# The columns of a widened source tile padded from 490 to 512, so that a matmul of the layers fills a whole PSUM bank

## The chip, the cores and the metric

The kernel runs on one core of one Trainium2 chip. The metric is the device time of one execution in microseconds; lower is better. The kernel before takes 4031.41 us (median of 3 runs, 4030.12 to 4032.72).

## What is computed

Two graph networks with a residual and a layer norm behind each. The change sits in the first, three graph convolutions on 6250 nodes and 200000 edges that are sorted by destination:

```python
def _graph_conv(x, W, b, src, dst, norm_src, norm_dst, n_nodes, act):
    h = x @ W
    m = h[src] * norm_src[:, None]
    agg = jax.ops.segment_sum(m, dst, num_segments=n_nodes)
    out = agg * norm_dst[:, None] + b
    return jax.nn.relu(out) if act else out
...
h = _graph_conv(feats, W1, b1, src, dst, norm_src, norm_dst, n, act=True)
h = _graph_conv(h, W2, b2, src, dst, norm_src, norm_dst, n, act=True)
h = _graph_conv(h, W3, b3, src, dst, norm_src, norm_dst, n, act=False)
...
x = _layernorm(x + _L0_gnn_ref(...), axis=-1)
```

The second network works per edge (two dense layers on a basis of the edge's weight, then a running product over the edges of a node) and comes behind the layers; the change does not touch it.

## The kernel before

The program has stages with a barrier between them: a stage that counts, a stage with the three layers, a stage on the edges, and a short end.

**What the layers work on.** The counting stage leaves a table of step counts in memory: for each of 49 source tiles of 128 nodes and each of 7840 steps (a step gathers up to 128 edges of one destination), how often each source node occurs in that step. Its entries are small whole numbers in bf16. One layer sums, for every step, the scaled node rows by these counts: a matrix product of `hp` (the node rows, 128 nodes x 128 features per source tile, as weights) with the counts (128 nodes x steps, moving). The steps are cut into `BLOCKS` = 16 blocks of `SB` = 490, the source tiles into `NG7` = 7 groups of 7. The counts of one block and one group, 7 tiles of 490 columns, are a **granule**; a layer has 112 of them, three layers 336.

**How a granule goes through.** SyncE loads it as bf16 into `gran`, a ring of 7 (`load_granule`, L738). Two engines widen it to 4 bytes (fp32r) into `wide`, a ring of `WIDE` = 2: VectorE its first `NEAR` = 4 tiles in one instruction (`widen`, L990), ScalarE the other 3 (`widen`, L823). TensorE then runs 14 matmuls (`granule`, L900): for each of the 7 tiles one for each of `PARTS` = 2 parts of `hp` (a rounded part and the rest that rounding leaves, so that the product keeps its precision). All 98 matmuls of a block add into one PSUM bank, `ybanks[n.parity()]`, of which 490 of the 512 columns are used. `s_un` says that the near tiles are used, `s_gran` that the granule is; on these VectorE and ScalarE wait before they write the slot again. `s_wn` and `s_wf` say that a slot is widened; on these TensorE waits.

**Behind a block.** VectorE scans the 490 sums into segment sums (L960), scales them (L964) and adds the bias (L969); TensorE multiplies by the layer's weights (`times_w`, L911, four fp32 matmuls of 128 columns, issued behind the first granule of the next block); ScalarE copies and stores the rows (L806, L813). GpSimd gathers each node's last row for the next layer (L796), VectorE scales it (L982), and ScalarE and VectorE split it into the two parts of `hp` (L829, L994). The opening of a layer runs granules of two blocks in an order of its own (`LEAD`), so that TensorE has work while the last node rows come in.

A row of `wide` for one tile is 490 x 4 = 1960 bytes long before and the next begins right behind it; tile 0 of slot 0 begins where the ring begins, which is the same place before and after.

Of the kernel before, what the change touches and what calls it, by code (L numbers as in the profile page):

```python
# [7 lines left out]
F32 = mybir.dt.float32  # L8
BF16 = mybir.dt.bfloat16
F32R = mybir.dt.float32r  # L10
# [4 lines left out]
P = 128  # L15
# [14 lines left out]
SB = 490  # L30
# [8 lines left out]
WIDE = 2  # L39
# [26 lines left out]
def gnn(nc, x, src, dst, edge_attr, edge_weight, w1, b1, w2, b2, w3, b3, v1, c1, v2, c2, v3, c3, out):  # L66
# [14 lines left out]
    with outer:  # L81
# [35 lines left out]
        with ExitStack() as ph:  # L117
            sbt = sb_in(ph)
# [104 lines left out]
            with nc.Block() as block:  # L223
# [263 lines left out]
                def _(act):  # L487
                    done = [0]

                    def tables(j):  # L490

                        n = RB[j + 1] - RB[j]
                        act.wait_ge(s_lo, j + 1)
                        if j:
                            act.wait_ge(s_tf, fills_to[j - 1])
                        nc.scalar.copy(lo_b[:, 0:n, :], lo_i[:, 0:n, :]).then_inc(s_lob, 1)
                        while done[0] < fills_to[j]:
                            f = done[0]
                            _, tab, a, b = fills[f]
                            act.wait_ge(s_tf, f + 1)  # L500
                            turned, n = banks[4 + f % TBANKS][:, 0:(b - a) * P], (b - a) * P
                            if tab == 0:
                                nc.scalar.copy(lo_t[:, a * P:b * P], turned).then_inc(s_te, 1)
                            else:
                                nc.scalar.copy(hi_t[:, a * P:b * P, :], turned.unsqueeze(2).to_broadcast([P, n, 2])  # L505
                                               ).then_inc(s_te, 1)
                            done[0] += 1
# [28 lines left out]
                def _(pe):  # L536
# [32 lines left out]
                    def turn_tables(j):  # L569

                        pe.wait_ge(s_lob, j + 1)
                        pe.wait_ge(s_hib, j + 1)
                        while done[0] < fills_to[j]:
                            f = done[0]
                            _, tab, a, b = fills[f]
                            if f >= TBANKS:
                                pe.wait_ge(s_te, f - TBANKS + 1)
                            for t in range(a, b):
                                last = nc.tensor.matmul(banks[4 + f % TBANKS][:, (t - a) * P:(t - a + 1) * P],
                                                        (lo_b, hi_b)[tab][:, t - RB[j], :], ident_b[:],  # L580
                                                        start=True, stop=True)
                            last.then_inc(s_tf, 1)
                            done[0] += 1
# [49 lines left out]
        with ExitStack() as ph:  # L633
            sbt = sb_in(ph)
            hps = sbt("hp", [P, NT, PARTS, D], F32R)
            hps_f = hps[:].bitcast(F32)
            gran = sbt("gran", [P, RING, 7, SB], BF16)
            wide = sbt("wide", [P, WIDE, 7, SB], F32R)
            by_tile = lambda ring, i, a, b: ring[:, i % RING, :, a * IS:b * IS].rearrange("p i (t s) -> p t i s", s=IS)
            in_runs = lambda i, a, b: wide[:, i % WIDE, a:b, 0:SB].rearrange("p t (i s) -> p t i s", s=IS)  # L640
            x_again = sbt("x_again", [P, 2, 7, D])
# [12 lines left out]
            ybanks, rbanks = banks[0:2], banks[2:4]  # L654
# [66 lines left out]
            def gathered(engine, q, k, last_too):  # L721
                early = 7 if q < 6 else LATE - 42
                engine.wait_ge(s_xg[q], 16 * early * k)
                if q == 6 and last_too:
                    engine.wait_ge(s_xl, 16 * (NT - LATE) * k)

            with nc.Block() as block:
# [159 lines left out]
                @block.tensor  # L887
                def _(pe):
                    def granule(k, n, g, i=None):
                        if g == 0:  # L890
                            pe.wait_ge(s_scan, n.value(1, 1))
                        y, r = ybanks[n.parity()][:, 0:SB], (n.parity() + g) % WIDE if i is None else i % WIDE
                        nth = n.value(7, g + 1) if i is None else i + 1
                        pe.wait_ge(s_wn, nth)
                        for t in range(7):
                            if t == NEAR:
                                pe.wait_ge(s_wf, nth)
                            for part in range(PARTS):
                                first, last_ = (g, t, part) == (0, 0, 0), (g, t, part) == (6, 6, PARTS - 1)
                                last = nc.tensor.matmul(y, hps[:, 7 * g + t, part, :], wide[:, r, t, :],  # L900
                                                        start=first, stop=last_)
                            if t == NEAR - 1:
                                last.then_inc(s_un, 1)
                        last.then_inc(s_gran, 1)

                    def times_w(k, m):
                        pe.wait_ge(s_scaled, m.value(1, 1))
                        pe.wait_ge(s_ho, m.value(1, 1))
                        rows = rbanks[m.parity()]
                        for t, a in enumerate((0, P, 2 * P, SB - P)):  # L910
                            last = nc.tensor.matmul(rows[:, t * D:(t + 1) * D], scaled[:, a:a + P], ws[k][:],  # L911
                                                    start=True, stop=True)
                        last.then_inc(s_z, 1)

                    pe.sem_inc(s_z, 1)

                    def one_block(k, n):
                        for g in range(NG7):
                            granule(k, n, g)
                            if g == 0:  # L920
                                times_w(k, n.plus(-1))

                    def opening(k):
                        for i, (b, g) in enumerate(LEAD):
                            if b == 0:
                                pe.wait_ge(s_hp, NG7 * k + g + 1)
                            granule(k, At(BLOCKS * k + b), g, NG7 * BLOCKS * k + i)
                            if i == 0:
                                times_w(k - 1, At(BLOCKS * k - 1))
                            if i == FIRST_DONE:  # L930
                                times_w(k, At(BLOCKS * k))

                    for k in range(3):
                        if k == 0:
                            for g in range(NG7):
                                pe.wait_ge(s_hp, g + 1)
                                granule(0, At(0), g)
                            pe.wait_ge(s_w, 16 * 6)
                            one_block(0, At(1))
                        else:  # L940
                            opening(k)
                        with pe.Fori(0, (BLOCKS - 2) // 2) as it:
                            for h in range(2):
                                one_block(k, At(BLOCKS * k + 2 + h, it, 2))
                    times_w(2, At(BLOCKS * 3 - 1))

                @block.vector
                def _(dve):
                    links = [0]

                    def link(ins):
                        links[0] += 1
                        ins.then_inc(s_link3, 1)
                        dve.wait_ge(s_link3, links[0])
# [23 lines left out]
                    def scale_h(k, q):  # L978
                        part = x_sb[:, 7 * q:7 * q + 7, :]
                        if k:  # L980
                            gathered(dve, q, k, True)
                        nc.vector.tensor_tensor(part, part, norm_src[:, 7 * q:7 * q + 7].unsqueeze(2).to_broadcast([P, 7, D]),  # L982
                                                ALU.mult).then_inc(s_hm, 1)
# [53 lines left out]
                    def normalise(i):  # L1037
# [4 lines left out]
                                                           ALU.subtract, ALU.mult)  # L1042
                        last.then_inc(s_x1, 1)

                    scale_h(0, 0)
                    scale_h(0, 1)
                    rest_h(0, 0)
# [62 lines left out]
        with ExitStack() as ph:  # L1110
            sbt = sb_in(ph)
# [310 lines left out]
        with ExitStack() as ph:  # L1422
            sbt = sb_in(ph)
# [168 lines left out]
```

## Time and profile before

| | |
|---|---|
| median of 3 runs | 4031.41 us (4030.12 to 4032.72) |
| the profiled execution: its own time | 4028.69 us |
| its span | 4026.8 us |
| mean granted TensorE clock over the span | 0.879 |
| TensorE busy | 3234.2 us, 80% of the span |
| matmuls of L900 | 4704 |
| time from the first to the last of them | 850.7 to 1945.0 us of the span |

The page gives busy time by engine, then 40 equal slices of the span (some 100.7 us each) with the busy tenths of each engine and the granted clock. The layers lie in slices 9 to 19. A busy TensorE is not a TensorE at its peak: matmuls are pipelined, a record lasts longer than the distance to the next one, and what a matmul costs is read from where one begins to where the next begins. A weight load (PEld) is recorded as beginning together with the matmul that runs beside it; its records are shorter than a matmul's turn in the layers, so the timeline can show them one by one, and the distance between two weight loads is read as the distance between two matmuls.

### The profile page before, as it was taken

The page shows a single profiled execution, that of the slowest core. Times are in us where ns is not written, and L with a number is a line of the kernel's source. Part 1 is how long each engine was busy: PE and PEld are TensorE (multiplying, and loading weights), DVE is VectorE, ACT ScalarE, POOL GpSimd, SP SyncE. Part 2 cuts the span into 40 slices and gives each one's busy share as a digit, 9 for nine tenths or more (in the row PEclk, how much of TensorE's full clock was granted, in tenths as well). Part 3 has the DMA queues.
Part 4 walks back from the last instruction along what each step waited for, and adds up shares of the span by engine and source line. Part 5 has one row for each costly group of instructions (what it writes and reads, how often), then busy time and mean ns, then how long its engine had stood idle before and what let it go on. Part 6 is the DMA issues. An engine that isn't in the chain of part 4 may idle for free. (4 is left out here: it accounts for less than half of the span.)

```text
span 4026.8 us, 61194 instructions
## 1 busy us (share of the span) xinstructions
PE 3234.2 (80%) x21477; PEld 2643.9 (66%) x21477; DVE 3228.0 (80%) x5075; ACT 2856.6 (71%) x3090; POOL 1934.6 (48%) x1883
## 2 busy tenths in 40 slices
PE   4898888879999999999677777777777777777763
PEld 3777777768888888888456555555555555555542
DVE  9999999964555545555599989898889889898896
ACT  3666666654445445444599999999999999999973
POOL 6122200042210121021477777777777777777774
PEclk7888888899999999999888888888888888888885
DMA  4444333379999999999587877777777777777762
GB/s 136 135 134 132 129 124 130 131 259 317 321 307 318 311 314 318 303 340 321 171 221 217 221 209 209 209 212 207 210 211 212 209 216 207 211 209 210 209 170 77
DMA packets 363341, 876.56 MB, mean 218 GB/s; under 512 B 54730, under 2 KB 213695, under 8 KB 363175
## 3 DMA queue, kind: packets, MB, share of 16 engines
q1 hardware_dynamic: 272471, 739.80, 57.5%
q0 software_dynamic: 59936, 119.71, 13.0%
q10 hardware_dynamic: 30768, 15.26, 1.3%
q8 instruction: 54, 0.88, 0.1%
q14 instruction: 112, 0.92, 0.1%
HBM read 653.46 MB, written 221.09 MB: 217 GB/s over the span
## 5 line engine op out<-in xcount | busy, mean ns | idle before, releaser
L1199 POOL DMA_INDIRECT hgat<-x_rows,edge_src x1564 | 1476.0, 944 | 485.5 <-issue 484.9
L900 PE MATMUL psum<-wide,hp 128*128 128x490 f32 x4704 | 1060.6, 386 | 15.5 <-DVE wide L990 14.2
L900 PEld LDWEIGHTS psum<-wide,hp 128*128 128x128 f32 x4704 | 884.5, 189 | 173.6 <-issue 15.1
L823 ACT CAST wide<-gran 128x1470 fp32r<-128x1470 bf16 x336 | 479.4, 1427 | 547.2 <-PE psum L900 538.7
L990 DVE CAST wide<-gran 128x1960 fp32r<-128x1960 bf16 x336 | 397.6, 1184 | 439.3 <-PE psum L900 431.8
L609 PEld LDWEIGHTS psum<-hi_hot,lo_hot 128*128 128x128 bf16 x7840 | 544.5, 155 | 216.4 <-issue 66.7
L1380 DVE TENSOR_SCALAR psum<-rows_e,edge_same,edge_first 128x128 f32<-128x128 f32 x1564 | 644.2, 412 | 42.4
L525 ACT CAST stage<-psum 128x490 bf16<-128x490 f32 x784 | 451.1, 575 | 306.3 <-PE psum L609 297.8
L609 PE MATMUL psum<-hi_hot,lo_hot 128*128 128x49 bf16 x7840 | 572.8, 219 | 93.4 <-DVE hi_hot L401 91.8
L1304 PE MATMUL psum<-c_b,one_b 96*128 96x512 bf16 x391 | 186.4, 477 | 507.1 <-DVE prod_e L1362 503.4
L796 POOL DMA_INDIRECT x_sb<-h_rows,last_i x147 | 179.7, 1223 | 856.3 <-DMA h_rows<-h_out 822.5
L1308 PEld LDWEIGHTS psum<-v_sb,excess 128*128 128x128 f32 x3128 | 543.9, 245 | 28.1
L398 DVE TENSOR_TENSOR lo_hot<-lo_t,rep_lo 128x8960 bf16<-128x8960 bf16 x112 | 539.4, 4816 | 5.0 <-ACT hi_t L505 4.5
L1308 PE MATMUL psum<-v_sb,excess 128*128 128x128 f32 x3128 | 537.0, 328 | 0.0
L1308 PE MATMUL psum<-v_sb,a 128*128 128x128 f32 x3128 | 513.8, 319 | 0.0
L1383 DVE TENSOR_TENSOR rows_e<-psum,prod_e 128x128 f32<-128x128 f32 x1564 | 455.1, 291 | 53.4
L1308 PEld LDWEIGHTS psum<-v_sb,a 128*128 128x128 f32 x3128 | 483.6, 235 | 0.0
L1304 PEld LDWEIGHTS psum<-c_b,one_b 96*128 96x128 bf16 x391 | 44.2, 113 | 666.0 <-DVE prod_e L1362 319.5
L1293 PE MATMUL psum<-dist,v_sb 128*128 128x512 f32 x782 | 374.4, 601 | 47.3 <-ACT dist L1225 25.5
L560 PE MATMUL psum<-stage,ident_b 128*128 128x490 bf16 x791 | 343.0, 435 | 0.2 <-ACT stage L525 0.2
L1256 ACT ACTIVATE a<-psum,soft_max 128x1024 f32<-128x1024 f32 x196 | 217.6, 1110 | 141.4 <-PE psum L1308 140.9
L1362 DVE TENSOR_TENSOR prod_e<-hgat,psum 128x1024 f32<-128x1024 f32 x196 | 238.8, 1218 | 87.4 <-issue 73.1
(218 smaller groups left out, 3667.7 us busy)
## 6 DMA issues: line engine op xcount, KB each, us to landing
gran<-step_counts SPq DMA_DIRECT2D x336, 857.5 KB, 6.6
dist<-weight_by_step SPq DMA_DIRECT2D x195, 512.0 KB, 6.7
running_products<-rows_e SPq DMA_DIRECT2D x195, 512.0 KB, 3.2
step_counts<-stage SPq DMA_DIRECT2D x112, 857.5 KB, 5.1
ef<-in_edge_attr SPq DMA_DIRECT2D x195, 448.0 KB
hgat<-x_rows,edge_src POOLq DMA_INDIRECT x1564
kn<-keep_and_norm_of_steps SPq DMA_DIRECT2D x48, 490.0 KB, 8.0
ef<-in_edge_attr SPq DMA_DIRECT2D x171, 64.0 KB
```

Of the source, the lines that this page charges most:

```text
L398: nc.vector.tensor_tensor(lo_hot[:, r], lo_of.unsqueeze(2).to_broadcast([P, 7, P, GS]), rep_lo[:].unsqueeze(1).to_broadcast([P, 7, P, GS]) ...
L525: nc.scalar.copy(stage[:, u % 2, :, g * GS:(g + 1) * GS], banks[f % 4][:, 0:GS * NT].rearrange("p (s h) -> p h s", h=NT)).then_inc(s_ev, 1)
L560: return nc.tensor.matmul(counts, ident_b[:], stage[:, r, :, g * GS:(g + 1) * GS], start=False, stop=False)
L609: last = nc.tensor.matmul(banks[f % 4][:, s * NT:(s + 1) * NT], lo_hot[:, u % 2, g, :, s], hi_hot[:, u % 2, g * GS + s, 0:NT], start=True, ...
L823: nc.scalar.copy(in_runs(i, NEAR, 7), by_tile(gran, i, NEAR, 7)).then_inc(s_wf, 1)
L900: last = nc.tensor.matmul(y, hps[:, 7 * g + t, part, :], wide[:, r, t, :], start=first, stop=last_)
L990: nc.vector.tensor_copy(in_runs(i, 0, NEAR), by_tile(gran, i, 0, NEAR)).then_inc(s_wn, 1)
L1199: pool.indirect_dma_start(out=hgat[:, f % U, c, :], out_offset=None, in_=x1_d, in_offset=bass.IndirectOffsetOnAxis(ap=edge_src[:, 2 * f + ...
L1293: last = nc.tensor.matmul(ps1[:, a:a + BLK], v1_sb[:], dist[:, f.ring(Q), a:a + BLK], start=True, stop=True)
L1308: last = nc.tensor.matmul(z[:, at:at + D], part[:, f.parity(), at:at + P], v2_sb[:], start=False, stop=part is a1 and c == C4 - 1)
L1380: nc.vector.tensor_scalar(factors[:, c], before, edge_same[:, b, c:c + 1], edge_first[:, b, c:c + 1], ALU.mult, ALU.add).then_inc(s_fac, 1)
L1383: nc.vector.tensor_tensor(rows_e[:, r, e, :], factors[:, c], prod_e[:, f % R, e, :], ALU.mult).then_inc(s_row if c < C4 - 1 else s_run, 1)
```

## The change

The rows of `wide` get 512 columns in place of 490. The last 22 of each of the 14 rows are set to zero once, by one VectorE instruction at the start of the layers; the widening goes on writing columns 0 to 489 only. `y` becomes the whole bank, and since the matmul takes `wide[:, r, t, :]`, it takes 512 columns in and writes 512. What reads the bank (L960) still reads 490 columns.

```diff
@@ -635,7 +635,7 @@
             gran = sbt("gran", [P, RING, 7, SB], BF16)
-            wide = sbt("wide", [P, WIDE, 7, SB], F32R)
+            wide = sbt("wide", [P, WIDE, 7, 512], F32R)
             by_tile = lambda ring, i, a, b: ring[:, i % RING, :, a * IS:b * IS].rearrange("p i (t s) -> p t i s", s=IS)
             in_runs = lambda i, a, b: wide[:, i % WIDE, a:b, 0:SB].rearrange("p t (i s) -> p t i s", s=IS)
@@ -889,7 +889,7 @@
                         if g == 0:
                             pe.wait_ge(s_scan, n.value(1, 1))
-                        y, r = ybanks[n.parity()][:, 0:SB], (n.parity() + g) % WIDE if i is None else i % WIDE
+                        y, r = ybanks[n.parity()], (n.parity() + g) % WIDE if i is None else i % WIDE
                         nth = n.value(7, g + 1) if i is None else i + 1
@@ -1042,6 +1042,7 @@
+                    link(nc.vector.memset(wide[:, :, :, SB:512].bitcast(F32), 0.0))
                     scale_h(0, 0)
                     scale_h(0, 1)
                     rest_h(0, 0)
```

No instruction changes its place. On VectorE, at the start of the layers, one instruction is added ahead of the first scaling of the node rows (L982), and the widening writes four runs of 490 where it wrote one of 1960:

```order
 L1005 MEMSET soft_max 128x1
 L1006 TENSOR_SCALAR center<-pcol 128x1
+L1045 MEMSET wide 128x14x22
 L982 TENSOR_TENSOR x_sb<-x_sb,norm_src 128x896 x2
 L994 TENSOR_TENSOR hp<-x_sb,hp 128x7x128
-L990 CAST wide<-gran 128x1960 x2
+L990 CAST wide<-gran 128x4x490 x2
```

The widening by ScalarE (L823) changes in the same way, from one run of 1470 to three of 490. On TensorE, at the start of the first layer, the count of the matmuls stays and their width changes:

```order
 L887 UNCONDITIONAL_BRANCH
-L900 MATMUL psum<-wide,hp 128x490 x112
+L900 MATMUL psum<-wide,hp 128x512 x112
 L911 MATMUL psum<-w,scaled 128x128 x4
-L900 MATMUL psum<-wide,hp 128x490 x84
+L900 MATMUL psum<-wide,hp 128x512 x84
```

So it goes on through all three layers.

## Rows read from the trace of the kernel before

**Rows 1.** The page: busy time of TensorE, and its 40 slices.
```profile
PE 3234.2 (80%) x21477; PEld 2643.9 (66%) x21477; DVE 3228.0 (80%) x5075; ACT 2856.6 (71%) x3090; POOL 1934.6 (48%) x1883
...
PE   4898888879999999999677777777777777777763
...
PEclk7888888899999999999888888888888888888885
```

**Rows 2.** Windows, the layers behind their first eight granules: busy time by engine, clock.
```profile
core 0: us, PE busy (x) PEld busy (x) DVE busy (x) ACT busy (x) POOL busy (x), PEclk, DMA share, GB/s
883.00:1945.00 1062.00, 1062.00 (x4959) 906.93 (x4958) 558.70 (x627) 506.60 (x389) 208.31 (x169) 1.00 0.93 315
```

**Rows 3.** Groups of instructions, 1000 to 1800 us, shapes apart.
```profile
line engine op names shapes xcount | busy us, mean ns | idle before us <-releasers
L900 PE MATMUL psum<-wide,hp 128*128 128x490 f32 x3457 | 777.9, 386 | 0.0
...
L823 ACT CAST wide<-gran 128x1470 fp32r<-128x1470 bf16 x247 | 352.4, 1427 | 398.1 <-PE psum L900 398.1
L990 DVE CAST wide<-gran 128x1960 fp32r<-128x1960 bf16 x247 | 292.2, 1184 | 330.2 <-PE psum L900 329.9
...
L994 DVE TENSOR_TENSOR hp<-x_sb,hp 128x896 fp32r<-128x896 f32 x14 | 15.3, 1091 | 13.7 <-ACT hp L829 13.7
...
L829 ACT CAST hp<-x_sb 128x896 fp32r<-128x896 f32 x14 | 13.2, 943 | 12.6 <-PE psum L900 10.9 <-DVE x_sb L982 1.8
```

**Rows 4.** Waits, 880 to 1945 us: who waited for whom, total, times, longest.
```profile
ACT wide L823 <- PE psum L900: 532.4, 315, 1.9
DVE wide L990 <- PE psum L900: 431.8, 252, 2.3
```

**Rows 5.** Timeline of weight loads: tile 0, then tile 1 of a slot-0 granule; next two granules.
```profile
1206.67 0.19 PEld L900 LDWEIGHTS psum<-wide,hp 128*128 128x128 f32 x1
1207.11 0.19 PEld L900 LDWEIGHTS psum<-wide,hp 128*128 128x128 f32 x1
1209.80 0.19 PEld L900 LDWEIGHTS psum<-wide,hp 128*128 128x128 f32 x1
1212.90 0.19 PEld L900 LDWEIGHTS psum<-wide,hp 128*128 128x128 f32 x1
```

**Rows 6.** Timeline of weight loads: second and sixth matmul of the layers, clock 0.50.
```profile
851.25 0.33 PEld L900 LDWEIGHTS psum<-wide,hp 128*128 128x128 f32 x1
852.88 0.33 PEld L900 LDWEIGHTS psum<-wide,hp 128*128 128x128 f32 x1
```

**Rows 7.** Windows of L900 alone, around those of group 6 (its columns: PE, PEld, PEclk).
```profile
851.20:853.30 2.10, 2.10 (x7) 1.66 (x6) 0.50 1.03 422
```

**Rows 8.** Timeline of weight loads, edge stage: two matmuls with 512 columns.
```profile
2989.37 0.19 PEld L1293 LDWEIGHTS psum<-dist,v_sb 128*128 128x128 f32 x1 [0.24 <-issue]
2989.80 0.19 PEld L1293 LDWEIGHTS psum<-dist,v_sb 128*128 128x128 f32 x1 [0.24 <-issue]
```

**Rows 9.** Windows, all engines, around those of group 8: the clock.
```profile
2988.00:2990.90 2.90, 2.82 (x14) 1.51 (x13) 2.73 (x7) 2.90 (x4) 1.99 (x4) 1.00 0.92 219
```

**Rows 10.** Timeline of VectorE at the start of the layers.
```profile
845.08 2.09 DVE L982 TENSOR_TENSOR x_sb<-x_sb,norm_src 128x896 f32<-128x896 f32 x2
847.32 1.10 DVE L994 TENSOR_TENSOR hp<-x_sb,hp 128x896 fp32r<-128x896 f32 x1
849.38 1.18 DVE L990 CAST wide<-gran 128x1960 fp32r<-128x1960 bf16 x1 [0.96 <-DMA gran<-step_counts]
```

**Rows 11.** Groups of VectorE's memsets: the two nearest in size.
```profile
L389 DVE MEMSET stage<- 128x1715 uint32 x1 | 1.5, 1488 | 0.3 <-issue 0.3
L1387 DVE MEMSET c_b<- 96x256 uint32 x1 | 0.3, 272 | 0.0
```

**Rows 12.** Timeline of TensorE: the first eight granules of the layers.
```profile
850.70 7.79 PE L900 MATMUL psum<-wide,hp 128*128 128x490 f32 x28 [12.80 <-DVE wide L990]
858.91 6.49 PE L900 MATMUL psum<-wide,hp 128*128 128x490 f32 x28 [0.43 <-DVE hp L994]
865.84 6.50 PE L900 MATMUL psum<-wide,hp 128*128 128x490 f32 x28 [0.44 <-DVE hp L994]
872.77 3.39 PE L900 MATMUL psum<-wide,hp 128*128 128x490 f32 x14 [0.42 <-DVE hp L994]
877.53 3.35 PE L900 MATMUL psum<-wide,hp 128*128 128x490 f32 x14 [1.37 <-DVE wide L990]
```

## The prediction, made before the changed kernel ran

> **What bounds the kernel now.** I began with the page [rows 1]. The change touches the layers alone; in its slices 10 to 19 TensorE is busy for nine tenths or more and its clock is granted in full. Next came the windows of that stage [rows 2]: from 883 to 1945 us TensorE is busy for 1062.00 of 1062.00 us, at clock 1.00 (2.4 GHz), while VectorE has 558.70 and ScalarE 506.60 us of work. Third the groups and waits [rows 3, 4]: the matmuls of L900 have no idle time before them, and both widening engines wait for these matmuls, 431.8 us in VectorE's case and 532.4 us in ScalarE's. So the stage lasts as long as its matmuls, and each nanosecond on one of the 4704 is a nanosecond on the end: behind the stage is a barrier, and nothing of the edge stage can start earlier.
>
> **What one matmul costs now.** A matmul's record (386 ns) is longer than its turn, so I read starts. In [rows 5] a granule of slot 0 begins at 1206.67 us, the next (slot 1) at 1209.80 and the third at 1212.90. That is 6.23 us for 28 matmuls, or **222.5 ns** each. Its columns alone are 490 / 2.4 GHz = 204.2 ns. So each matmul has some **18.3 ns** that no column explains. At the start of the stage the clock is 0.50 (1.2 GHz) [rows 7], and there four matmuls take 852.88 - 851.25 = 1.63 us [rows 6], 407.5 ns each. The columns alone are 490 / 1.2 GHz = 408.3 ns there, so at half clock the surplus is gone. Two things follow: columns are paid one by one (490 are not rounded up to 512, which would be 427 ns), and the surplus belongs to something that only shows at full clock. What that is no row tells, and the forecast turns on what it does at 512 columns.
>
> **The change part by part.**
>
> *Twenty-two columns more in each of 4704 matmuls.* If the surplus stays as it is, a matmul costs 22 / 2.4 GHz = 9.17 ns more, 231.7 ns, and all of them 4704 x 9.17 = **43.1 us**. If it grows with the columns (a stream that comes in at a slower rate than one column per cycle), a matmul costs 222.5 x 512 / 490 = 232.5 ns, 10.0 ns more: 47.0 us. If it is gone at 512, the nearest row with that width sets the end: L1293 at full clock moves 512 columns of fp32, two cycles for each, from 2989.37 to 2989.80 us [rows 8, 9], 0.43 us, where 1024 cycles are 0.427 us; 3 ns of surplus. By that a matmul of L900 would cost 213.3 + 3 = 216 ns, 6.5 ns less than now: 4704 x 6.5 = 30.6 us off. I take 43.1 us: the row at half clock is of the same instruction and shows columns paid one by one, while L1293 reads its columns at half the speed, so the surplus of L900 need not show there in any case.
>
> The Trainium skill's page "TensorE: Matmul & The Clock Gate", section "Back-to-back issue gap", speaks against that choice: it gives N / 2.4 + 2.5 ns for one matmul behind another, and 215.7 ns as measured at 512 columns. For 490 columns that rule makes 206.7 ns, which [rows 5] does not bear out (222.5); for 512 it makes 215.8 ns and so 4704 x 6.7 = 31.5 us off, were the padded rows to run by it.
>
> *The first eight granules.* These are 112 of the 4704 matmuls, and TensorE waits between them for node rows and for loaded granules [rows 12]. What they lengthen (112 x 9.17 = 1.0 us) can partly go into those waits: between 0 and 1.0 us of the 43.1. I leave it in.
>
> *One memset of 14 x 22 = 308 columns, and a wait for it.* [Rows 11] give 272 ns for 256 columns and 1488 ns for 1715, so some 0.85 ns a column: about 0.32 us, at most twice that for short runs and the wait. It delays L982 and L994 behind it, but L990 then waits 0.96 us for the first granule's load [rows 10], and the first matmul needs L990. Cost 0; if the load came earlier, at most 0.6 us.
>
> *Widening into runs of 490.* L990 takes 1184 ns and L823 1427 ns [rows 3], of a granule's 3.1 us. Writing with gaps is seen on L829, 943 ns for 896 elements, 1.05 ns each against L823's 0.97: at that rate L823 takes 1.55 us. For VectorE the bad end is the pace of L994 (1091 / 896 = 1.22 ns): L990 would take 2.39 us, 1.2 us more. VectorE waits 431.8 / 336 = 1.29 us a granule for TensorE [rows 4], so even that is covered on average, and 336 x 1.2 = 403 us on its 558.70 leaves it at 962 of 1062 us. Cost 0; the bad end is priced below. The granules' loads change by nothing: TensorE takes them 4% more slowly.
>
> Sum: +43.1 us on the profiled execution's 4028.69 us is 4071.8 us. The median of the runs lies 2.7 us above that execution, so for the median I say 4031.41 + 43.1 = **4074.5 us**, 1.07% slower.
>
> **The rivals.**
>
> *A, the forecast: columns are paid.* 43.1 us, with bounds 34 (alignment gives back 2 ns of 9) and 47: 4065 to 4079 us.
>
> *B, the surplus comes from rows that begin anywhere, and goes.* Tiles are 1960 bytes apart now, so of the 14 rows of the ring most begin off any larger boundary; padded to 2048 bytes all begin alike. If the read of a row that begins badly costs the 18.3 ns, the change ends at 216 ns a matmul: 4031.41 - 30.6 = 4000.8 us. It turns to a gain once more than 9.2 of the 18.3 ns go. For it: the surplus is real, shows only at full clock, where columns are read fastest, and the two slots differ (3.13 and 3.10 us, [rows 5]), as they also do in where their rows begin. Against it: tile 0 of slot 0 already begins where it begins after the change, and its two matmuls take 1207.11 - 1206.67 = 0.44 us, 220 ns each; a well-placed start saves some 2 ns, not 18. The loads can follow that pace too: DMA's share of 0.93 would be 0.96 [rows 2]. The Trainium skill's page "SBUF — State Buffer", section "Specifications (TRN2)", has a rule for this rival: memory is read in lines of 16 bytes and each step to a new line costs something. Half of the rows begin inside such a line now, none afterwards; [rows 5] shows no such step at tile 0.
>
> *C, the 512 columns are there already.* If whatever feeds the array works in pieces of 64 or 128 columns, 490 cost it as much as 512 at full clock, and the surplus is the rest of the last piece: 222.5 ns stay, 4031.4 us. For it: 512 / 2.4 = 213.3 ns plus a few for the start comes near 222.5, and at half clock the array, not the feed, would be the limit, as [rows 6] has it. Against it: no row shows steps by pieces.
>
> *D, VectorE loses its pace* in L990 and is late behind each block, where L960, L964 and L969 also stand: 48 blocks with up to 1 us each on top of A, up to 4122 us. For it: the output is no longer one run. Against it: the 1.29 us of waiting per granule.
>
> That the change does not do what it says I set aside: the matmuls have 512 columns in all three layers.
>
> **How the numbers follow.** A 0.74, B 0.12, C 0.11, D 0.03. The predicted time is A's. A's own range is 4065 to 4079 us; with up to 5 us for casts that are now and then late, 4084. A alone is less than 8 in 10, so the range goes down to take in C with its scatter, 4028 us; B and D are left out. A change below 0.2% (8 us) cannot be told from none here: faster is B, 0.12; same is C, 0.11; slower A and D, 0.77.
>
> **What would show it.** Right: the distance of matmuls of L900 near 231.7 ns (3.24 us a granule) at clock 1.00, the span from first to last grown by 43 us, TensorE without gaps, the waits of VectorE and ScalarE for L900 longer by some 40 us each, L990 and L823 as long as before, and stages before and behind unchanged. Wrong: a distance near 216 ns (B) or 222.5 ns (C), or idle time before L900 put down to L990 (D).

## The result

| | median, us | ratio to before, 95% interval |
|---|---|---|
| before | 4031.55 (4030.12 to 4032.72, 4 runs) | |
| the change | 4084.76 (4084.43 to 4086.60, 4 runs) | 1.0132 [1.0120, 1.0144] |

The change costs 53.2 us. Forecast were 43.1 us, and a range that ended at 4084.0 us. The sign and the mechanism were right, a term of some 10 us was missing, and the time lies 0.8 us above the end of the range.

### The profile page after: what moved, and what is told of

Same layout as the page of the kernel before. It is cut to its first block and busy times, and to the rows that moved or that the text cites. A ratio compares the mean times of both kernels' runs of the same rounds, so it can differ in the third digit from the quotient of the medians.

```text
span 4082.6 us, 61195 instructions
## 1 busy us (share of the span) xinstructions
PE 3292.7 (81%) x21477; PEld 2647.0 (65%) x21477; DVE 3232.0 (79%) x5076; ACT 2858.4 (70%) x3090; POOL 1943.4 (48%) x1883
## 5 line engine op out<-in xcount | busy, mean ns | idle before, releaser
L900 PE MATMUL psum<-wide,hp 128*128 128x512 f32 x4704 | 1116.3, 398 | 13.7 <-DVE wide L990 12.9
L900 PEld LDWEIGHTS psum<-wide,hp 128*128 128x128 f32 x4704 | 883.6, 189 | 227.2 <-issue 13.6
L823 ACT CAST wide<-gran 128x1470 fp32r<-128x1470 bf16 x336 | 479.7, 1428 | 598.5 <-PE psum L900 591.8
L990 DVE CAST wide<-gran 128x1960 fp32r<-128x1960 bf16 x336 | 397.6, 1184 | 483.2 <-PE psum L900 478.3
```

The source lines that it names most:

```text
L823: nc.scalar.copy(in_runs(i, NEAR, 7), by_tile(gran, i, NEAR, 7)).then_inc(s_wf, 1)
L990: nc.vector.tensor_copy(in_runs(i, 0, NEAR), by_tile(gran, i, 0, NEAR)).then_inc(s_wn, 1)
```

## The profile after

The view by windows, from behind the first granules to the last matmul (core 0; columns as in [rows 2]):

```profile
883.00:1998.00 1115.00, 1115.00 (x4955) 904.65 (x4954) 561.74 (x627) 506.94 (x389) 215.24 (x169) 1.00 0.90 300
```

TensorE still has no gap and full clock, as in [rows 2]; VectorE and ScalarE have the same work as before. So the layers are as long as their matmuls, as forecast. The matmul's own group, by the view of line L900 (minimum, median and maximum duration in ns, first and last start):

```profile
L900 PE MATMUL psum<-wide,hp x4704: 392/397/767, 850.5 to 1998.7; 128*128 128x512 f32 x196
```

From first to last start it is 1148.2 us; before it was 850.7 to 1945.0, 1094.3 us: 53.9 us more. L900 begins at the same time to within 0.2 us, and what lies behind it takes 4082.6 - 1998.7 = 2083.9 us against 4026.8 - 1945.0 = 2081.8. So 53.9 of the 55.8 us between the two spans are in L900, and some 2 us lie behind it.

Weight loads on the timeline, as in [rows 5]: the first matmuls of three granules in a row, slot 0, slot 1, slot 0:

```profile
990.78 0.19 PEld L900 LDWEIGHTS psum<-wide,hp 128*128 128x128 f32 x1
994.06 0.19 PEld L900 LDWEIGHTS psum<-wide,hp 128*128 128x128 f32 x1
997.34 0.19 PEld L900 LDWEIGHTS psum<-wide,hp 128*128 128x128 f32 x1
```

6.56 us for 28 matmuls: **234.3 ns** each, where 231.7 was forecast and 222.5 stood before. Both slots now take the same 3.28 us, which the slots before did not (3.13 and 3.10 us). Over its columns (512 / 2.4 = 213.3 ns) a matmul now has 21.0 ns, 2.7 ns more surplus than before. At half clock, weight loads five matmuls apart, and the window of L900 around them:

```profile
850.62 0.34 PEld L900 LDWEIGHTS psum<-wide,hp 128*128 128x128 f32 x1
852.75 0.33 PEld L900 LDWEIGHTS psum<-wide,hp 128*128 128x128 f32 x1
```

```profile
850.60:854.00 3.40, 3.40 (x8) 2.69 (x9) 0.50 1.04 419
```

That is 426 ns each, and 512 / 1.2 is 426.7: no surplus there, as before.

The small terms came out as forecast. VectorE's timeline at the start of the layers, and the widening groups (1000 to 1800 us, shapes apart):

```profile
844.82 0.32 DVE L1045 MEMSET wide<- 128x308 f32 x1
845.17 2.09 DVE L982 TENSOR_TENSOR x_sb<-x_sb,norm_src 128x896 f32<-128x896 f32 x2
847.27 1.09 DVE L994 TENSOR_TENSOR hp<-x_sb,hp 128x896 fp32r<-128x896 f32 x1
849.05 1.29 DVE L990 CAST wide<-gran 128x1960 fp32r<-128x1960 bf16 x1 [0.69 <-DMA gran<-step_counts]
```

```profile
L823 ACT CAST wide<-gran 128x1470 fp32r<-128x1470 bf16 x235 | 335.5, 1428 | 414.3 <-PE psum L900 414.3
L990 DVE CAST wide<-gran 128x1960 fp32r<-128x1960 bf16 x235 | 277.9, 1183 | 346.4 <-PE psum L900 346.3
```

The memset takes the 0.32 us of the estimate, and L990 still waits behind it for the load [rows 10]. The casts into runs of 490 cost what they cost before (1428 and 1183 ns, [rows 3]). Waits of 880 to 1990 us, as in [rows 4]:

```profile
ACT wide L823 <- PE psum L900: 582.2, 316, 2.0
DVE wide L990 <- PE psum L900: 478.0, 260, 2.4
```

They grew by 49.8 and 46.2 us: the added time lands as waiting on the widening engines.

## The experiments

Two theories on the missing 10 us stood at the start: the surplus grows with the columns (**rate**), or it is fixed for each matmul and the new row starts made it larger (**starts**). Distances below are means over the starts of matmuls inside granules in the trace, and good to some 0.2 ns; the rows shown are first matmuls of granules, 14 matmuls apart. The kernels whose layers differ from each other, and the one with rows 496 columns apart, ran once; of them the distances are read, layer by layer, and not the time. In the code, `...` marks lines or ends of lines that are left out.

### The change taken apart: pitch and width

Pitch 512 with 490 columns (against the changed kernel):

```diff
-y, r = ybanks[n.parity()], ...
+y, r = ybanks[n.parity()][:, 0:SB], ...
...
-    last = nc.tensor.matmul(y, hps[:, 7 * g + t, part, :], wide[:, r, t, :],
+    last = nc.tensor.matmul(y, hps[:, 7 * g + t, part, :], wide[:, r, t, 0:SB],
```

> The rows stay 512 columns apart and padded, but the matmul takes 490 columns again. If the feed runs at a slower rate than one column per cycle (a matmul of the changed kernel takes 3.280 us / 14 = 234.3 ns for 512 columns, 0.4576 ns each), a matmul takes 224.2 ns, 1.8 ns more than before, and the kernel some 8 us more than the 4031.5 us before: 4040 us. If the surplus is fixed and the new row starts have raised it from 18.2 to 21.0 ns, a matmul takes 204.2 + 21.0 = 225.1 ns and the kernel 4044 us. If row starts do not matter and the surplus is fixed, 222.4 ns and 4031.5 us.

Measured: 4019.19 us (8 runs), before 4030.92, ratio **0.9971 [0.9960, 0.9982]**: 11.7 us *less* than before. Weight loads on its timeline:

```profile
986.68 0.19 PEld L900 LDWEIGHTS psum<-wide,hp 128*128 128x128 f32 x1
989.76 0.19 PEld L900 LDWEIGHTS psum<-wide,hp 128*128 128x128 f32 x1
992.85 0.19 PEld L900 LDWEIGHTS psum<-wide,hp 128*128 128x128 f32 x1
```

6.17 us for 28 matmuls, 220.4 ns by these rows and 220.0 by the starts in the trace, equal in both slots. None of the three numbers expected was this low. The padded rows by themselves help, by 2.5 ns a matmul.

Pitch 490 with 512 columns:

```diff
-wide = sbt("wide", [P, WIDE, 7, 512], F32R)
+wide = sbt("wide", [P, WIDE, 7 * SB + 22], F32R)
...
-                            if t == NEAR:
+                            if t == NEAR - 1:
                                 pe.wait_ge(s_wf, nth)
...
-    last = nc.tensor.matmul(y, hps[:, 7 * g + t, part, :], wide[:, r, t, :],
+    last = nc.tensor.matmul(y, hps[:, 7 * g + t, part, :], wide[:, r, t * SB:t * SB + 512],
...
```

> The rows are 490 columns apart as before the change, and the matmul takes 512, the last 22 of which belong to the next tile (behind the last tile stand zeros); what falls into columns 490 to 511 of the bank is read by nobody. TensorE waits for ScalarE's tiles one tile earlier. If the surplus is fixed and depends on row starts, a matmul takes 213.3 + 18.2 = 231.5 ns and the kernel 4031.5 + 43 = 4075 us. If only the number of columns counts, 234.3 ns as in the changed kernel, and 4085 us.

Measured: 4073.65 us (4 runs), ratio **1.0106 [1.0090, 1.0123]**, 42.7 us more than before. Its timeline:

```profile
991.64 0.19 PEld L900 LDWEIGHTS psum<-wide,hp 128*128 128x128 f32 x1
994.89 0.19 PEld L900 LDWEIGHTS psum<-wide,hp 128*128 128x128 f32 x1
998.13 0.19 PEld L900 LDWEIGHTS psum<-wide,hp 128*128 128x128 f32 x1
```

6.49 us for 28: 231.8 ns by these rows and 231.9 by the starts, near the 231.5 of the fixed surplus. The four kernels side by side:

| ns a matmul (us in all) | 490 columns | 512 columns | 22 columns cost |
|---|---|---|---|
| rows 490 apart | 222.5 (4030.92) | 231.9 (4073.65) | 9.4 |
| rows 512 apart | 220.0 (4019.19) | 234.3 (4084.76) | 14.3 |

In each of the four the distance is the same in all three layers to 0.2 ns. On rows 490 apart the columns cost 42.7 us, against 43.1 forecast. The pitch alone gives 11.7 us at 490 columns and **takes** 10.5 us at 512 (53.2 less 42.7, each against the runs of the kernel before that were made beside it). That is the missing term: not the columns, but what the rows' new places do to a matmul of 512. One thing more differs in the kernel with 512 columns on rows 490 apart: its last 22 columns hold counts of the next tile where the changed kernel has zeros. No run separates the two.

### How the surplus goes with the width

Widths by layer, on padded rows (three kernels, `COLS` is the only difference between them, and each has one of its three lines):

```diff
+COLS = (448, 480, 504)
+COLS = (496, 500, 508)
+COLS = (256, 320, 384)
+OFF = (0, 0, 0)
...
-y, r = ybanks[n.parity()], ...
+y, r = ybanks[n.parity()][:, 0:COLS[k]], ...
...
-    last = nc.tensor.matmul(y, hps[:, 7 * g + t, part, :], wide[:, r, t, :],
+    last = nc.tensor.matmul(y, hps[:, 7 * g + t, part, :], wide[:, r, t, OFF[k]:OFF[k] + COLS[k]],
```

> Padded rows; the matmuls of the first layer take 448 columns, those of the second 480, those of the third 504, so the sums of the columns behind are left out. Read is the distance of matmuls inside a granule. A slower rate of the feed: 205.0, 219.6 and 230.6 ns. A fixed surplus of 21.0 ns: 207.6, 221.0 and 231.0 ns. A feed in pieces of 64 columns: 205.0, 234.3 and 234.3 ns.

> Padded rows, widths 496, 500 and 508 by layer, more than the 490 that anyone reads, so nothing is left out. Known on these rows: 490 columns 220.0, 504 columns 226.9, 512 columns 234.3 ns. If the price rises evenly between those points: 222.9, 224.9 and 230.6 ns. If it rises in steps (of 16 columns, 6.67 ns): 220 or 226.7 for 496 and 500, and 226.9 or 234.3 for 508. If only the full 512 columns, a whole bank, are dear: 228.5 for 508.

> Padded rows; the matmuls of the first layer take 256 columns, those of the second 320, those of the third 384, so the sums of the columns behind are left out, and TensorE will wait for loads between granules. Read is the distance inside a granule. Known on these rows: 448 columns 200.0 ns (480 cycles of 2.4 GHz), 490 columns 220.0 ns (528), 508 columns 226.7 ns (544). If the surplus is fixed for each matmul (32 to 40 cycles): 120 to 123, 147 to 150 and 173 to 177 ns. If the 4-byte columns come in at a slower rate (480 / 448 = 1.071 cycles each): 114.3, 142.9 and 171.4 ns.

From the timelines, layer with 448 columns, then the one with 508, then 384 (one kernel each; 28 matmuls between the two rows of a pair):

```profile
975.90 0.19 PEld L902 LDWEIGHTS psum<-wide,hp 128*128 128x128 f32 x1
...
981.50 0.19 PEld L902 LDWEIGHTS psum<-wide,hp 128*128 128x128 f32 x1
```

```profile
1718.81 0.19 PEld L902 LDWEIGHTS psum<-wide,hp 128*128 128x128 f32 x1
...
1725.16 0.19 PEld L902 LDWEIGHTS psum<-wide,hp 128*128 128x128 f32 x1
```

```profile
1597.83 0.19 PEld L902 LDWEIGHTS psum<-wide,hp 128*128 128x128 f32 x1
...
1602.69 0.19 PEld L902 LDWEIGHTS psum<-wide,hp 128*128 128x128 f32 x1
```

5.60 us, 6.35 us and 4.86 us for 28: 200.0, 226.8 and 173.6 ns (200.0, 226.7 and 173.3 by the starts in the trace). All widths on padded rows, in ns and in cycles of 2.4 GHz:

| columns | 320 | 384 | 448 | 480 | 490 | 496 | 500 | 504 | 508 | 512 |
|---|---|---|---|---|---|---|---|---|---|---|
| ns | 146.7 | 173.3 | 200.0 | 217.1 | 220.0 | 223.3 | 223.4 | 226.9 | 226.7 | 234.3 |
| cycles | 352 | 416 | 480 | 521 | 528 | 536 | 536 | 544 | 544 | 562 |
| less the columns | 32 | 32 | 32 | 41 | 38 | 40 | 36 | 40 | 36 | 50 |

(At 256 columns most distances were 115 to 120 ns, and TensorE waited for loads.) The rate theory falls: it wanted 142.9 ns at 320 and 171.4 at 384. On these rows the surplus is 32 cycles from 320 to 448 columns and 36 to 41 from 480 to 508; near the top the measured widths fit steps of 8 columns (496 and 500 cost the same, 504 and 508 too), so that there a column more is not always paid. Only 512 stands apart: one step above 508 would be 552 cycles, 230.0 ns; it takes 4.3 ns more. The staircase is not a matter of the width alone: in the opening of the first layer eight granules of 496 columns ran at 226.7 ns a matmul, a step higher than the 223.3 behind the next `times_w`.

### What the surplus is made of

> Padded rows, 512 columns in all layers. First layer: only 64 of the 128 weight columns are loaded, so half of the features are left out. Second layer: weights and moving columns are bf16 (constant weights, the first half of a row read as bf16). Third layer: the loads are cut to 70 columns and both widenings to 2 columns, so that next to nothing but TensorE touches the memory. Read is the distance of matmuls inside a granule. If the surplus comes from 4-byte columns that the feed delivers too slowly: 234.3, 216, 234.3 ns. If it comes from the weight load that runs beside each matmul: clearly under 234.3 ns (near 224) in the first layer, 234.3 in the third. If it comes from the other engines' and the DMA's traffic: 234.3, 216 to 234, and 216 ns in the third.

```diff
+if k == 0:
+    last = nc.tensor.matmul(y[0:64], hps[:, 7 * g + t, part, 0:64], wide[:, r, t, :],
...
+elif k == 1:
+    last = nc.tensor.matmul(y, hb[:], wide[:, r, t, :].bitcast(BF16)[:, 0:512],
...
+else:
...
+small = i >= 2 * BLOCKS * NG7
+nc.vector.tensor_copy(wide[:, i % WIDE, 0, 0:2] if small else in_runs(i, 0, NEAR),
...
...
+sp.dma_start(gran[:, i % RING, 0:1, 0:70], p_rows[g, :, b, 0:1, 0:70]
...
```

The bf16 layer, then the layer with little traffic, weight loads 28 matmuls apart, and the windows of both (all engines, columns as in [rows 2]):

```profile
1355.87 0.10 PEld L912 LDWEIGHTS psum<-wide,hb 128*128 128x128 bf16 x1
...
1361.92 0.10 PEld L912 LDWEIGHTS psum<-wide,hb 128*128 128x128 bf16 x1
...
1719.64 0.19 PEld L915 LDWEIGHTS psum<-wide,hp 128*128 128x128 f32 x1
...
1726.20 0.19 PEld L915 LDWEIGHTS psum<-wide,hp 128*128 128x128 f32 x1
```

```profile
1300.00:1500.00 200.00, 199.40 (x960) 95.35 (x959) 101.49 (x94) 95.72 (x74) 37.48 (x29) 1.00 0.96 322
1620.00:1820.00 200.00, 200.00 (x894) 162.38 (x893) 39.44 (x115) 16.73 (x68) 20.76 (x22) 1.00 0.25 56
```

With bf16 weights and columns 6.05 us for 28, 215.8 ns by the starts, 2.5 ns over the columns. This layer also reads half the bytes in each row, so it does not say whether the type or the bytes take the surplus away. With VectorE busy for 39 of 200 us and DMA for a quarter, 6.56 us again, 234.3 ns: cutting the other engines' traffic changed nothing. With 64 weight columns the mean was 229.3 ns, 5.0 less than with 128; it is a mean of two prices, 226.6 and 231.7 ns, that take turns every seven granules.

> As the changed kernel, 512 columns. First layer: only 32 of the 128 weight columns, so three quarters of the features are left out. Second layer: all 14 matmuls of a granule load the same weights. Third layer: the weights begin 32 bytes off. If the surplus is partly time in which the weight load takes the memory (64 columns gave 229.3 ns instead of 234.3): near 226.8 ns in the first layer, 234.3 in the others, since the amount of weights is the same. If it hangs on which addresses of weights and columns meet: the second or third layer moves by some ns as well. If the weight load has no part in it and the 229.3 was chance: 234.3 ns in all three.

```diff
+rows, both = y, hps[:, 7 * g + t].rearrange("p a d -> p (a d)")
+if k == 0:
+    rows, weights = y[0:32], hps[:, 7 * g + t, part, 0:32]
+elif k == 1:
+    weights = hps[:, 7 * g, 0, :]
+else:
+    weights = both[:, 120 * part + 8 * (1 - part):120 * part + 8 * (1 - part) + 128]
...
```

Measured: 230.6 ns with 32 weight columns, so less weight does not go on helping; 234.3 with the same weights for all; 230.0 with the weights 32 bytes off (the first part 32 bytes on, the second 32 bytes back), their number unchanged. The rows of that third layer, 28 matmuls apart:

```profile
1748.81 0.19 PEld L907 LDWEIGHTS psum<-wide,hp 128*128 128x128 f32 x1
...
1755.25 0.19 PEld L907 LDWEIGHTS psum<-wide,hp 128*128 128x128 f32 x1
```

6.44 us for 28. So the 4.3 ns on top at 512 depend on where the weights lie as well as on where the columns lie; the 40 cycles stay.

### Where rows begin

> Padded rows 512 columns apart, matmuls with 490 columns that begin 8 columns (32 bytes) into the row in the first layer, 2 columns (8 bytes) in the second, 4 (16 bytes) in the third; so each matmul takes the counts of steps 8, 2 or 4 further on and some zeros. Read is the distance inside a granule; it was 220.0 ns from the row's own start. If where a row begins decides the surplus: 220.0 or less for one of the starts, and 222 ns or more for the 8-byte start, since the rows 1960 bytes apart took 222.5 ns on average. If it is only that all rows begin alike: 220.0 ns for all three.

```diff
+COLS = (490, 490, 490)
+OFF = (8, 2, 4)
...
-    last = nc.tensor.matmul(y, hps[:, 7 * g + t, part, :], wide[:, r, t, :],
+    last = nc.tensor.matmul(y, hps[:, 7 * g + t, part, :], wide[:, r, t, OFF[k]:OFF[k] + COLS[k]],
```

Measured: 220.0, 220.0 and 223.3 ns. An 8-byte start costs nothing; a 16-byte start does, at times. That a row begins badly, by itself, was not the surplus.

The 223.3 of the third layer is a mean of two prices, 220.0 and 226.7 ns. They take turns every seven granules, and the turn comes at the matmuls of `times_w` (L911, here L913). Two such stretches on TensorE's timeline, 98 matmuls each:

```profile
1624.14 1.05 PE L913 MATMUL psum<-w,scaled 128*128 128x128 f32 x8
1624.96 22.45 PE L902 MATMUL psum<-wide,hp 128*128 128x490 f32 x98
1647.24 1.05 PE L913 MATMUL psum<-w,scaled 128*128 128x128 f32 x8
1648.05 21.82 PE L902 MATMUL psum<-wide,hp 128*128 128x490 f32 x98
```

Both slots and all seven groups of source tiles have one price within a stretch. And the very same granule can have either: the third group of source tiles, in slot 0 and with the same PSUM bank, in the opening of this layer and then two blocks later (first matmul, and the first of the next granule, 14 further on):

```profile
1583.21 0.19 PEld L902 LDWEIGHTS psum<-wide,hp 128*128 128x128 f32 x1
1586.29 0.19 PEld L902 LDWEIGHTS psum<-wide,hp 128*128 128x128 f32 x1
...
1628.21 0.19 PEld L902 LDWEIGHTS psum<-wide,hp 128*128 128x128 f32 x1
1631.39 0.19 PEld L902 LDWEIGHTS psum<-wide,hp 128*128 128x128 f32 x1
```

3.08 us and then 3.18 us for 14 matmuls (220.0 and, by the starts, 226.7 ns each), with weights, columns and bank in the same places. So the price is not set by the addresses alone, but also by something that the interruption by `times_w` leaves behind; what that is no run shows.

> Rows 528 columns apart, 512 columns from the row's start in the first layer, 8 columns (32 bytes) in for the second, 2 columns (8 bytes) in for the third; the second and third layer take shifted counts. If the start decides: one of the three clearly under 234.3 ns, and the spread of the rows 490 apart (231.9 ns on average at 512 columns) shows here, some starts at 229 and some at 234. If the number of columns alone decides: 234.3 ns in all three.

```diff
+OFF = (0, 8, 2)
...
-wide = sbt("wide", [P, WIDE, 7, 512], F32R)
+wide = sbt("wide", [P, WIDE, 7, 528], F32R)
...
-    last = nc.tensor.matmul(y, hps[:, 7 * g + t, part, :], wide[:, r, t, :],
+    last = nc.tensor.matmul(y, hps[:, 7 * g + t, part, :], wide[:, r, t, OFF[k]:OFF[k] + 512],
...
```

Measured: 233.8, 230.5 and 231.7 ns. The start decides over some 3 ns here, and the row's own start is the dearest of the three.

> Padded rows, 490 columns from the row's start, and the weights begin 32 bytes off in the first layer, 64 in the second, 128 in the third (the two parts are then no longer cut at their border, so the sums are of mixed features). The price so far follows columns rounded down to a multiple of 8, plus 40 cycles of 2.4 GHz: 488 + 40 = 528 cycles, 220.0 ns. If this is all there is at 490 columns: 220.0 ns in all three. If weights and columns still get into each other's way there, as they do at 512, one start falls by one or more steps of 8 cycles, to 216.7 ns or less, and a better kernel than both follows from it.

```diff
...
+both, off = hps[:, 7 * g + t].rearrange("p a d -> p (a d)"), (8, 16, 32)[k]
+at = 128 - off if part else off
-    last = nc.tensor.matmul(y, hps[:, 7 * g + t, part, :], wide[:, r, t, :],
+    last = nc.tensor.matmul(y, both[:, at:at + 128], wide[:, r, t, 0:SB],
```

Measured: 221.7, 220.1 and 220.1 ns (the second part of the weights is moved back by as much as the first is moved on). Nothing below 220.0; the 32 bytes that helped at 512 cost 1.7 ns here.

> Rows 496 columns (1984 bytes) apart, 490 columns from the start in the first layer, 2 and 4 columns in for the second and third (which take shifted counts). If any even pitch does: 220.0 ns in the first layer. If it takes rows that lie 2048 bytes apart: 221 to 224 ns, as with rows 1960 bytes apart (222.5). A fall below 220.0 ns in one of the layers would beat the pitch of 512.

Against the kernel before:

```diff
-wide = sbt("wide", [P, WIDE, 7, SB], F32R)
+wide = sbt("wide", [P, WIDE, 7, 496], F32R)
...
-    last = nc.tensor.matmul(y, hps[:, 7 * g + t, part, :], wide[:, r, t, :],
+    last = nc.tensor.matmul(y, hps[:, 7 * g + t, part, :], wide[:, r, t, 2 * k:2 * k + SB],
...
+link(nc.vector.memset(wide[:, :, :, SB:496].bitcast(F32), 0.0))
```

Measured: 222.9, 222.8 and 222.8 ns, no better than rows 1960 bytes apart. An even pitch by itself is not it; of the pitches tried, only 2048 bytes gave 220.0.

> The changed kernel with 32 unused bytes ahead of the ring of widened tiles, so that its rows begin 32 bytes further on, and nothing else. If the last 4.3 ns of the 234.3 come from the addresses at which rows and weights meet (with the weights 32 bytes off it was 230.1 ns): 512 + 40 = 552 cycles, 230.0 ns a matmul, 4.3 x 4704 = 20 us less than the changed kernel, 4064.5 us. If 512 columns cost 234.3 ns wherever they lie: 4084.8 us.

```diff
+ahead = sbt("ahead", [P, 8])
 wide = sbt("wide", [P, WIDE, 7, 512], F32R)
```

Measured: 4081.72 us (4 runs), ratio 1.0127 [1.0110, 1.0144]. Its timeline, 28 matmuls apart:

```profile
991.28 0.19 PEld L901 LDWEIGHTS psum<-wide,hp 128*128 128x128 f32 x1
...
997.82 0.19 PEld L901 LDWEIGHTS psum<-wide,hp 128*128 128x128 f32 x1
```

6.54 us, 233.6 ns by these rows and 233.4 by the starts: neither the 230.0 of the one theory nor the 234.3 of the other. Moving the rows by 32 bytes is not the same as moving the weights by 32 bytes. It does not settle whether only the distance between the two matters, since the weights had their two parts moved in opposite directions. **Open** is the rule: that the places cost up to 4.3 ns at 512 columns is measured, but not which places cost what, nor what `times_w` switches.

## Why the prediction was right and wrong

- *TensorE's matmuls set the length of the layers*: right. No gap, full clock, and 53.9 us of growth between the first and the last matmul of L900 in the profiled executions, against 53.2 us between the medians.
- *Columns are paid one by one, and the surplus of 18.3 ns stays*: right in its size for the width by itself on rows 490 apart, 231.9 ns and 42.7 us against 231.7 and 43.1 forecast. Half clock showed columns paid one by one, as [rows 6] have it (426 ns at 512 columns). At full clock on padded rows they are not: 496 and 500 columns cost the same, and the surplus is 15.8 ns at 490 columns and 21.0 at 512. That it came out as 18.3 on the mixed starts is in part luck; no run shows why. Rivals B and C fell: the padded matmul is far from 216 and from 222.5 ns. Of B's effect 2.5 ns are there, at 490 columns. The proportional bound of 47.0 us came closer to the total, but by chance; the rate behind it fell in the widths 320 and 384.
- **The step that failed** is the term for the place of the rows. The prediction let alignment only give back ("alignment gives back 2 ns of 9"), and put A's dear end at 47 us by the proportional rate, with nothing for a place that is dear. From [rows 5] it read tile 0 of slot 0 as 220 ns (221.5 by the starts in the trace) and took this as what a well-placed start saves. At 490 columns padded rows do give that (220.0 ns, 11.7 us less). At 512 the same row starts cost 2.4 ns a matmul more than the mixed starts of before: some 11 us by these distances, and by the times the 10.5 us that stand between 42.7 and 53.2. A surplus that had been measured at one width on fourteen different starts was carried to another width on one kind of start, with no bound for the case that this one is a dear one.
- *Memset and casts cost nothing*: right, 0.32 us under a wait for the load, and 1428 and 1183 ns as before. Rival D did not come.
- On the rule that spoke against the forecast: the N / 2.4 + 2.5 ns of the Trainium skill's page "TensorE: Matmul & The Clock Gate", section "Back-to-back issue gap", make an estimate of 215.8 ns for 512 columns, and that is what bf16 took here (215.8 ns). For the 4-byte columns of this kernel with 128 weight columns no run came near it: 230.0 ns was the least.
- The 16-byte lines of the Trainium skill's page "SBUF — State Buffer", section "Specifications (TRN2)", which stood behind rival B: rows that begin 8 bytes off, inside such a line, took 220.0 ns like those 32 bytes off, so that rule did not show in this read.

The best kernel is half of the change: rows 512 apart, and a matmul of 490 columns, 4019.19 us, 0.29% [0.18, 0.40] under before.

## What to carry to other kernels

A change that pads a row changes two things, the distance of the rows and the work on each; try them one at a time, since here the distance alone gains 11.7 us, and the 22 columns lose 42.7 us without it and 65.6 behind it. Zero columns were not free here (14.3 ns a matmul for 22 of them on padded rows), so pad the memory and not the matmul. When a surplus over the ideal is unexplained, it is no constant to carry to another shape: put a bound on both sides of it from its spread over the places that were measured.

## What the runs showed of the hardware that was not expected

- On rows 2048 bytes apart and at full clock an fp32r matmul took its columns plus 32 cycles of 2.4 GHz (13.3 ns) at 320 to 448 columns, and plus 36 to 41 (about 16 ns) at 480 to 508, where the measured widths fit steps of 8 columns; a bf16 matmul of 512 columns took 2.5 ns over its columns. At half clock (490 and 512 columns) the surplus is not seen.
- With 128 weight columns, 512 fp32r columns took 230.0 to 234.3 ns by where rows and weights lay, and 490 took 220.0 to 223.3, as means of a layer. With the other engines' traffic cut, 512 columns took the same 234.3.
- The same matmuls on the same addresses took 220.0 or 226.7 ns each for whole stretches of seven granules, and changed from one to the other at four matmuls of another kind between them.
